# Late expert weights asked for on ScalarE's queue during the expert phase, and four batches' outputs on the sync queue

## The reference

```
x = x + tanh(g_xattn) * attention(layernorm(x), ctx, W, b)     # x: 8 batches x 256 tokens x 256, float32
x = x + tanh(g_ffn)   * moe(layernorm(x), expert_sel, keys, values)

moe(xf):                                   # 2048 tokens
  sel = sigmoid(xf @ expert_sel.T)         # 64 experts
  the 4 best experts of each token, gate = sel there
  out = sum over chosen experts: gate * (relu(xf @ keys[e]) @ values[e])
                                           # keys[e] 256 x 128, values[e] 128 x 256, float32
```

## Time and profile before

| | |
|---|---|
| median of 3 runs | 254.44 us (251.56, 254.44, 255.45) |
| profiled execution | 251.02 us |
| its span | 249.2 us |
| granted TensorE clock, mean | 0.88 of full speed |
| busy PE / POOL / DVE / ACT | 179.5 / 139.5 / 130.3 / 109.2 us |
| DMA | 66.01 MB, mean 265 GB/s |

### The profile page before, as it was taken

How to read it: one execution, slowest core, us unless ns; L and a number is a source line. 1 busy time by engine, 2 the same in 40 slices (tenths; PEclk the granted TensorE clock), 3 DMA queues, 4 the chain that set the end, 5 groups by cost and what they waited for, 6 DMA issues and landing times.

```text
span 249.2 us, 4485 instructions
## 1 busy us (share of the span) xinstructions
PE 179.5 (72%) x1292; PEld 137.3 (55%) x1292; DVE 130.3 (52%) x496; ACT 109.2 (44%) x307; POOL 139.5 (56%) x156
## 2 busy tenths in 40 slices
PE   2999799689576340005999999999999995009773
PEld 2866576466453110005788888887777772007552
DVE  4568899977885752001112122356656561606584
ACT  2677978778766400001445445454545443000111
POOL 4003777777777777600577767777777777700000
PEclk9999999999995555555999999999999999657998
DMA  5899999999999999997589956675567522169996
GB/s 157 241 298 323 355 315 348 370 337 346 321 300 326 346 290 318 367 329 216 170 222 366 312 165 199 209 227 159 170 197 211 163 70 84 66 229 416 395 417 247
DMA packets 40894, 66.01 MB, mean 265 GB/s; under 512 B 5381, under 2 KB 24603, under 8 KB 40864
## 3 DMA queue, kind: packets, MB, share of 16 engines
q1 hardware_dynamic: 32572, 46.68, 60.3%
q0 software_dynamic: 6624, 16.82, 19.4%
q10 hardware_dynamic: 1668, 2.17, 2.4%
HBM read 38.31 MB, written 28.64 MB: 269 GB/s over the span
## 4 chain that ended last, share of the span: by engine, by line
PE 44%; DMA 14%; POOL 13%; DVE 12%; issue 10%; SPq 3%; ACT 3%; POOLq 1%; ACTq 0%; DVEq 0%
PE bank L746 13%; PE bank L775 12%; POOL x_slots L514 11%; DMA keys_sb<-y_rows 7%; PE bank L740 5%; SPq L475 3%; DMA x_slots<-rows,pos_i 3%; POOL y_rows L524 2%; PE bank L556 2%; PE bank L765 2%; PE bank L781 2%; DMA rows<-x_slots 2%; PE bank L628 2%; DVE shared L1288 1%; DMA bq_rows<-in_L_xattn_b 1%
## 5 line engine op out<-in xcount | busy, mean ns | idle before, releaser
L524 POOL DMA_INDIRECT y_rows<-rows,by_place x74 | 73.8, 997 | 39.1 <-ACT rows L1037 21.4
L514 POOL DMA_INDIRECT x_slots<-rows,pos_i x64 | 62.9, 982 | 38.1 <-DVE pos_i L1110 20.2
L1023 ACT COPY xT<-bank 128x512 f32<-128x512 f32 (+1 forms) x38 | 21.8, 574 | 59.3 <-PE bank L740 59.2
L1288 DVE TENSOR_SCALAR shared<-bank 128x256 f32<-128x256 f32 (+1 forms) x38 | 15.9, 417 | 54.9 <-PE bank L746 44.2
L740 PE MATMUL bank<-ident,rows 128*128 128x128 f32 x148 | 22.8, 279 | 20.8 <-DMA rows<-x_slots 20.8
L746 PE MATMUL bank<-xT,keys_sb 128*128 128x128 f32 x256 | 37.5, 288 | 0.0
L746 PEld LDWEIGHTS bank<-xT,keys_sb 128*128 128x128 f32 x256 | 33.1, 195 | 6.2 <-ACT xT L1023 3.3
L775 PE MATMUL bank<-values_sb,shared 128*128 128x256 f32 x128 | 35.1, 391 | 1.2 <-DVE shared L1288 1.2
L740 PEld LDWEIGHTS bank<-ident,rows 128*128 128x128 f32 x148 | 18.0, 146 | 21.7 <-issue 21.7
L1037 ACT COPY rows<-bank 128x512 f32<-128x512 f32 (+1 forms) x38 | 21.8, 575 | 18.2 <-PE bank L775 13.9
L775 PEld LDWEIGHTS bank<-values_sb,shared 128*128 128x128 f32 x128 | 21.4, 190 | 6.6 <-DVE shared L1288 3.1
(11 more groups left out here) (141 smaller groups left out, 300.4 us busy)
## 6 DMA issues: line engine op xcount, KB each, us to landing
x_slots<-values_sb SPq DMA_DIRECT2D x4, 2056.0 KB, 29.9
rows<-x_slots SPq DMA_DIRECT2D x64, 128.5 KB, 4.2
keys_sb<-y_rows SPq DMA_DIRECT2D x16, 512.0 KB, 9.6
values_sb<-in_L_ffn_values SPq DMA_DIRECT2D x5, 1024.0 KB, 13.9
xs<-in_x SPq DMA_DIRECT2D x8, 256.0 KB, 8.3
out<-xs ACTq DMA_DIRECT2D x7, 256.0 KB, 6.2
values_sb<-in_L_ffn_values SPq DMA_DIRECT2D x1, 1408.0 KB
rows<-x_slots SPq DMA_DIRECT2D x40, 32.1 KB
```

The lines of the kernel that those rows point to most:

```text
L514: pool.indirect_dma_start(x_slots, bass.IndirectOffsetOnAxis(ap=pos_i[:, t * K + k:t * K + k + 1].bitcast(U32), axis=0), rows[:, t % RB * ...
L524: pool.indirect_dma_start(y_rows, bass.IndirectOffsetOnAxis(ap=result_at[:, t:t + 1], axis=0), y_sb[:, t % R, :], None, bounds_check=last_ ...
L1023: act.copy(xgT[:, 2 * ring + part.start:2 * ring + part.stop, :].rearrange("p u d -> p (u d)"), pT(place_of(part, ring))[:, part.start * D ...
L1288: dve.tensor_scalar(hidT[:, 2 * ring + part.start:2 * ring + part.stop, :].rearrange("p u n -> p (u n)"), pH(place_of(part, ring))[:, part ...
```

## The change

Three of the five late loads leave SP's queue. ACT asks for them instead, in four DMAs, each right behind the copies of a turn of the expert phase: keys 40 to 47 in turn 1 (with a wait for a_S in front), keys 48 to 55 in turn 3, keys 56 to 63 in turn 5, and values 50 to 60 in turn 7. The number of late loads becomes 6. Values 40 to 49 and 61 to 63 stay on SP, in the same place. In the end stage the outputs of batches 0 to 3 (HELD = 4) are asked for by SP, behind its 16 result loads; ACT does not wait for their tiles any more. The functions that ask for late weights now take the engine as an argument.

```diff
--- before.py
+++ after.py
@@ -85,9 +85,10 @@
     PAIR = 2 * M
     PT = 2 * TB
     ADDED = (1, 3, 6, 8, 10, 12, 14)
+    HELD = 4
     LATE = 24
     FREE_KEYS, FREE_VALUES = 56, (50, 61)
-    LATE_LOADS = 5
+    LATE_LOADS = 6
     assert (D, M <= P, F, C, TB, E, N * K) == (2 * P, True, P, 2, 2, 64, 8192)
     assert R == PAIRS * V and TILES % 2 == 0 and REST % PAIRS == 0 and Q * (QUADS + REST * V) >= UNITS
     assert ALONE + MIXED.count("e") == E and E - LATE >= ALONE and ALONE % R == 0 and MIXED[:2] == "ee"
@@ -341,6 +342,15 @@
                 skip_runtime_bounds_check_because="they are sums over one expert's number at most")[1]
             return [experts[Q * n:Q * n + Q] for n in range(quads)]
 
+        k_src = keys.rearrange("e (c p) f -> p (e c) f", p=P)
+        v_src = values.rearrange("e f d -> f e d")
+
+        def late_keys_in(eng, first, last):
+            eng.dma_start(keys_sb[:, first * C:last * C, :], k_src[:, first * C:last * C, :]).then_inc(late_in, 16)
+
+        def late_values_in(eng, first, last):
+            eng.dma_start(values_sb[:, first:last, :], v_src[:, first:last, :]).then_inc(late_in, 16)
+
         def rest_turns(eng, turn, used):
 
             with eng.If(used > 0):
@@ -368,21 +378,12 @@
                 tokens_in(2 * n)
                 tokens_in(2 * n + 1)
 
-            k_src = keys.rearrange("e (c p) f -> p (e c) f", p=P)
-            v_src = values.rearrange("e f d -> f e d")
-
             def weights(n):
                 sp.dma_start(keys_sb[:, n * C:(n + 8) * C, :], k_src[:, n * C:(n + 8) * C, :]).then_inc(weights_in, 16)
                 sp.dma_start(values_sb[:, n:n + 8, :], v_src[:, n:n + 8, :]).then_inc(weights_in, 16)
 
             for n in range(0, E - LATE, 8):
                 weights(n)
-
-            def late_keys_in(first, last):
-                sp.dma_start(keys_sb[:, first * C:last * C, :], k_src[:, first * C:last * C, :]).then_inc(late_in, 16)
-
-            def late_values_in(first, last):
-                sp.dma_start(values_sb[:, first:last, :], v_src[:, first:last, :]).then_inc(late_in, 16)
 
             sp.wait_ge(padding_ok, 2)
             for e in range(0, E, FE):
@@ -429,10 +430,6 @@
                         load_blocks(t, at_rows[q:q + Q])
                         q += Q
 
-            late_keys_in(FREE_KEYS, E)
-            late_values_in(*FREE_VALUES)
-            sp.wait_ge(a_S, T)
-            late_keys_in(E - LATE, FREE_KEYS)
             sp.wait_ge(a_O, T)
             sp.wait_ge(padded, 16 * E // FE)
             sp.wait_ge(r_first, 1)
@@ -441,8 +438,8 @@
                 sp.wait_ge(scattered[n], 16 * K * len(range(n, T, RB)))
             for first in range(0, 2 * R, R):
                 turn_alone(first, first_rows[first:first + R])
-            late_values_in(E - LATE, FREE_VALUES[0])
-            late_values_in(FREE_VALUES[1], E)
+            late_values_in(sp, E - LATE, FREE_VALUES[0])
+            late_values_in(sp, FREE_VALUES[1], E)
             for first in range(2 * R, ALONE, R):
                 turn_alone(first)
             sp.wait_ge(r_first, 2)
@@ -473,6 +470,13 @@
 
             for t in range(T):
                 sp.dma_start(yg[:, t, :], y_tiles[:, t, :]).then_inc(yg_in[t], 16)
+            for b in range(HELD):
+                for t in range(TB * b, TB * (b + 1)):
+                    if t in ADDED:
+                        sp.wait_ge(y_added, ADDED.index(t) + 1)
+                    else:
+                        sp.wait_ge(y_mixed, mixed_at[t])
+                sp.dma_start(out_tiles[:, b, :, :], xs[:, TB * b:TB * (b + 1), :]).then_inc(out_done, 16)
             sp.wait_ge(out_done, 16 * (B + 1))
 
         @block.gpsimd
@@ -1051,6 +1055,15 @@
                     results_out(At(p), p % 2, part)
                 for n in rows_of[1:]:
                     rows_out(At(n), n % RING)
+                if p == 1:
+                    act.wait_ge(a_S, T)
+                    late_keys_in(act, E - LATE, (E - LATE + FREE_KEYS) // 2)
+                if p == 3:
+                    late_keys_in(act, (E - LATE + FREE_KEYS) // 2, FREE_KEYS)
+                if p == 5:
+                    late_keys_in(act, FREE_KEYS, E)
+                if p == 7:
+                    late_values_in(act, *FREE_VALUES)
             used = rest_used(act)
 
             def turn(p, quad):
@@ -1067,12 +1080,14 @@
 
                 for part in ([slice(0, TB)] if b < B - 1 else [slice(0, 1), slice(1, TB)]):
                     tiles = range(TB * b + part.start, TB * b + part.stop)
-                    for t in tiles:
-                        if t in ADDED:
-                            act.wait_ge(y_added, ADDED.index(t) + 1)
-                        else:
-                            act.wait_ge(y_mixed, mixed_at[t])
-                    act.dma_start(out_tiles[:, b, part, :], xs[:, tiles.start:tiles.stop, :]).then_inc(out_done, 16)
+                    if b >= HELD:
+                        for t in tiles:
+                            if t in ADDED:
+                                act.wait_ge(y_added, ADDED.index(t) + 1)
+                            else:
+                                act.wait_ge(y_mixed, mixed_at[t])
+                    if b >= HELD:
+                        act.dma_start(out_tiles[:, b, part, :], xs[:, tiles.start:tiles.stop, :]).then_inc(out_done, 16)
 
         @block.vector
         def _(dve):
```

## The result

| | before | changed |
|---|---|---|
| median, first comparison | 253.49 us (251.56 to 255.45, 4 runs) | 259.83 us (256.71 to 261.09, 4 runs) |
| ratio to before | | 1.0207, 95% interval 1.0119 to 1.0295 |
| median, another chip (changed_c) | 251.19 us (13 runs) | 261.81 us (4 runs), ratio 1.0324 (1.0198 to 1.0451) |
| median, a third of the chips (changed_d) | 251.42 us (11 runs) | 259.41 us (6 runs), ratio 1.0265 (1.0190 to 1.0339) |
| profiled execution, its span | 251.02 us, 249.2 us | 261.09 us, 259.0 us |

The change made the kernel 2 to 3% slower. The forecast was 253 us, and the range ended at 258.5. The medians are over all executions; the ratios leave out the slow ones (more than 1.5% above the fastest of their kernel), and the traces of the changed kernel here, of changed_c and of half_dose_c are of such executions. Where sizes matter, several traces are set side by side.

The account below looks back on a forecast made before the run. Bounds: POOL's scatters and two transfers in front, POOL again in the expert phase, result loads at the end. Terms -6.1 + 6.6 + 1.0 - 1.8 = -0.3 us, so 252.7, given as 253; range 246 to 258.5.

Parts of the forecast that it names:

- the stall: Expert phase, turn 8: TensorE waits for tiles 20 and 21 behind SP's late values, slowed by ACT's loads; +6.6 us.
- The upper bound of 9.5: Turn 8: the longest wait of TensorE allowed for, 9.5 us, with DMA at 357 GB/s and POOL at 100.
- Rival 1: Expert phase: SP's values are not starved, tiles 20 and 21 land in time; 245.1 us, chance 0.28.
- The front joint: Front stage: without late loads the last scatter lands 4.0 us sooner and the first gather 2.1; -6.1 us, bounds -2 and -6.5.
- rival 3: Front stage gains little: first gather keeps 4.2 us, scatter lands in 4.4; 256.8 us, chance 0.10.
- The clock: After the wait in turn 8: the clock falls to the 1.2 GHz level and products slow; +1.0 us (0 to 2).
- The requests on ACT: Expert phase, turns 1 to 7: key requests hold ACT 0.9 to 1.5 us, values 5.5; all hidden, nothing on the path.
- Rival 2: Expert phase: ACT is held at its requests, about 13 us in turn 7, kernel slower; 258.5 to 262.3 us, chance 0.16.
- The end stage: End: with outputs behind the result loads the last load lands sooner; -1.8 us, bounds 0 and -2.2.

Follow-up runs that it names:

- changed_c: The changed kernel run again, unaltered, on another chip: 261.81 us, ratio to before 1.0324.
- changed_d: The changed kernel run again, unaltered, with more rounds on a third of the chips: 259.41 us, ratio to before 1.0265.
- half_dose_c: Changed kernel with keys 56 to 63 and values 50 to 60 back on SP in the front stage: 253.50 us, ratio to before 1.0044.
- only_end: The kernel before with only the end-stage part of the change (SP asks for outputs of batches 0 to 3): 249.90 us, ratio 0.9999.
- free_in_front: Changed kernel, keys 56-63 and values 50-60 on SP in front, other late loads on ACT in turns 1, 4, 7, 10: 246.66 us on a normal-speed chip.
- all_on_act: Changed kernel with SP's 13 experts of late values also asked for on ACT, in turns 9 and 11: 247.50 us, ratio to before 0.9906.
- act_values_11: Changed kernel with ACT's values request moved from turn 7 to 11: 294.66 us, ratio 0.9945 on a slow chip; 257.21 us, 1.0231 on a normal one.

## Why the prediction was wrong

The mechanism and its place were right; the main term, the stall, was half of what it measured, since the time of SP's own values beside ACT's loads was put at 15.3 us and was 21.5. So a forecast of no change met a kernel 2 to 3% slower. The difference of the two spans, 9.8 us, can be written in the prediction's own steps. The need of tiles 20 and 21 is put 0.89 us behind the start of the products before them, as in the earlier trace rows (137.62, 138.51).

| step | forecast | traces |
|---|---|---|
| start of POOL's last x_slots scatter | 0 | +1.87 (103.67 to 105.54) |
| from there to the first product | -6.1 | -6.03 (10.93 to 4.90) |
| first product to the need of tiles 20 and 21 | 0 | +0.15 |
| stall in turn 8 | +6.6 | +12.81 (134.50 to 147.31) |
| from there to POOL's last y_rows scatter (clock) | +1.0 | +2.18 (78.05 to 80.23) |
| from there to the end of the span | -1.8 | -1.18 (32.64 to 31.46) |
| sum | -0.3 | +9.8 |

**The stall, the term that failed.** The steps were that SP has moved 1.17 MB of its values by 133.4, and that "0.79 MB at about 170 GB/s last 4.6 us, to 138.0, and about 1 us passes until they have landed". That puts the last of the values at 136.5, 15.3 us after their request at 121.2, and the gathers of tiles 20 and 21 2.5 us behind. In the trace the values took 21.5 us (123.58 to 145.08) and the gathers 2.2 behind them. So the gathers were priced well, and the 6.2 us that the stall was longer are those of the values. By the packets they have three parts.

- By 12.2 us after the request SP had moved 1.00 MB of values and not 1.17. Up to 129 us 0.52 MB of gathers, those of tiles 16 to 19, still stood ahead of them in SP's queue, where the forecast has none, and the values moved at 71 GB/s.
- POOL's scatters got 90 GB/s from 129 to 134 us (0.45 MB) and not the 60 taken for them. So the others got less: SP's queue 96 (103 forecast) and ACT's 186 (207). All together had 372 (370).
- A mean rate is no rate for the last engine. At 141.1 us 0.21 MB of values were left, which is 1.2 us at q1's rate of 168 GB/s. They took 4.0, and 0.46 MB of gathers from behind them moved in the same time. So about 2.8 of the 6.2 us are the engines that were behind, and about 3.4 the rates before; both are estimates from these packets.

ACT's values beside the gathers are 1.0 us of the wait by the landings, and some 1.5 to 2.3 by the waits and the ratios. The upper bound of 9.5 was made with the same mean rate, so it was no bound; worked through the prediction's own steps with 357 and 100 GB/s it comes to about 10.5, which is still below 12.8. A warning lay in the trace before. Rival 1 has SP's values through 7.5 us after their request and the gathers of tiles 20 and 21 some 3 us ahead of their need. By the packets the values took 9.3 us, and the gathers were 0.7 us ahead.

**The front joint.** Both landings came out as priced, 2.44 and 2.14 us against 2.40 and 2.1, so rival 3 did not happen. But -6.1 is the gain against an execution in which POOL ends as early as in the earlier trace rows. In only_end POOL's last scatter of x_slots started at 109.18 us, and there the joint took 6.72 us (109.18 to 115.90), so by an estimate that execution would gain 1.8. POOL's first scatter started between 21.8 and 27.3 us in the traces of all kernels here, and the prediction took one execution's 21.90 for all of them. This may be part of why free_in_front gains 4.5 us and not 6; no run separates it.

**The clock.** Priced at +1.0 by one group of eight products, the stretch behind the stall took 2.18 us longer: the transposes, the products with the values and those with the keys behind the stall all ran at the lower level (1.11, 1.91 and 1.91 us).

**The requests on ACT.** The keys were right (0.9 to 1.5 forecast, 0.69 to 0.81 measured). The values were forecast to hold ACT for 5.5 us and held it for 1.38, hidden by the stall as said. The rows of SP they came from the earlier trace rows were of a queue that was full for the whole front stage. Rival 2 did not happen in the changed kernel; the kernel is slower by the forecast's mechanism, and not by that rival's. It did happen in all_on_act, with 3.52 us. Two requests at the same moment are in the trace as well: ACT's for keys at 123.48 us and SP's for values at 123.58 overlap, and they took 0.72 and 0.55 us, no longer than others.

**The end stage.** Forecast -1.8, -1.18 in the traces, and nothing in the times (ratio 0.9999, so within 0.9 us). The last DVE step came 2.3 us earlier behind the first result load (27.47 us before, 25.18 after). But 3.36 us and not 2.24 pass from it to the end of the span, while SP's outputs drain.

**Rival 1** (no starvation) was excluded by the first trace. Its time, 245.1 us, was the median of no kernel here (the given range, from 246, left it out too); free_in_front, in which no gather was late, came to 246.66.

**A reading of the rows.** That no mixed stretch of the trace before is above 380 GB/s does not hold: from 234 to 237 us q1 and q10 moved 0.83 and 0.40 MB, which is 410. The forecast did not rest on it, and the 370 that it took for the expert phase was right (372).

## What to carry to other kernels

A load that is moved to another engine's queue does not leave the road: it moved as many packets there as the other full queue, and what it slows is whatever stands at the end of that queue. Before moving a bulk load, look for bulk loads that stay on the old queue ahead of small transfers with a deadline, and move those too (0.9906 and 0.9845 here, against 1.02 to 1.03). Price such a bulk load by its last packet and not by a mean rate, count what stands ahead of it and every other queue that is busy, and look in the trace before how far ahead of its need the first small transfer behind it lands: here it was 0.7 us. And when several loads count on one semaphore, take their landings from something that tells them apart.

## What the runs showed of the hardware

- Two full queues shared the DMA engines by packets and not by bytes: 437 to 437 packets, 0.44 to 0.87 MB in 5 us, and 234 to 228 packets, 0.83 to 0.40 MB, in the earlier trace rows.
- The parts of two gathers behind a bulk load landed 6.4 us apart in the changed kernel, beside a second bulk load (140.89 to 147.26 us; 6.5 in changed_c), against 2.1 us in the kernel before. Rows of later gathers moved in that time, 6.4 tiles of them from 141.1 to 147.3 us. In free_in_front_c, with ACT's load alone beside them, tiles 20 and 21 landed 5.3 us apart too (127.60 to 132.91 us, 31 steps in the trace), but ahead of their need.
- Two of the chips ran every kernel some 18% slower (before at 296 and 299 us against 250 to 253). Why they are slower is open. In their traces engines wait between instructions for nothing that the profile shows, as ahead of ACT's copies in act_values_11 (busy us, mean ns, then idle us before them with what ended it; 14.0 us of it is put down to "issue", a wait for nothing that the profile shows, and 15.4 to "remote", which the view does not explain). In the changed kernel's trace the same group has 68.1 us of idle time, nearly the same sum, with 0.8 of it on "issue".

```profile
L1027 ACT COPY xT<-bank 128x512 f32<-128x512 f32 (+1 forms) x38 | 21.9, 575 | 69.8 <-PE bank L744 40.3 <-remote 15.4 <-issue 14.0
```

There the fault hardly showed: with ACT's values in turn 11 the ratio was 0.9945 and 0.9878, against 1.0231 and 1.0185 on the others. I read it so that TensorE asked for its tiles later there; a stall that hangs on a deadline depends on how fast the rest runs.
